# Router logits in pieces, W banks turned, and a new order of attention's work on five engines

## What is computed

```python
x = x + xattn(layernorm(x), ctx)          # q,k,v,o projections, softmax over 154 columns, 16 heads
h = layernorm(x)
w = softmax(h @ W_router.T + b_router)    # (tokens, 8)
w = keep_top_2(w)                         # the other six are zero
x = x + sum_e w[:, e] * (h @ W_experts[e].T + b_experts[e])
```

## Time and profile before

| what | us |
|---|---|
| median of three executions | 1285.32 |
| lowest, highest | 1275.66, 1287.61 |
| the profiled execution, first to last instruction | 1340.9 |
| PE busy in it | 1224.7 |
| DVE, ACT, POOL busy in it | 881.3, 722.1, 744.6 |
| one slot of attention in it, 175 to 220 us | 44.6 |
| one slot of attention in it, 420 to 471 us | 50.7 |

### The profile page before, as it was taken

The page is one execution under the profiler, slowest core; times in us unless marked ns, Lnnn a source line. Parts: engine busy times, 40 slices in busy tenths (PEclk is TensorE's granted clock), DMA queues, the critical chain, the costliest instruction groups (busy, mean ns, idle before and its releaser), DMA issues. The chain is left out here.

```text
span 1340.9 us, 36001 instructions
## 1 busy us (share of the span) xinstructions
PE 1224.7 (91%) x11024; PEld 735.1 (55%) x11025; DVE 881.3 (66%) x1933; ACT 722.1 (54%) x1040; POOL 744.6 (56%) x980
## 2 busy tenths in 40 slices
PE   8887999998999989999999986869899999999997
PEld 4445665655655655665655654534354555555454
DVE  4657787877868867867877867545445555555454
ACT  4336875775775775775766662624333333334333
POOL 4003555675675675675675674864644445444545
PEclk9879999999989998989989997889999999999999
DMA  8842664584583574583583573967999989998886
GB/s 267 253 135 65 173 176 153 148 254 142 150 258 130 142 241 152 147 262 131 144 237 115 132 215 109 357 221 156 199 177 184 175 173 188 179 172 155 168 165 133
DMA packets 135547, 239.22 MB, mean 178 GB/s; under 512 B 18440, under 2 KB 49416, under 8 KB 134280
## 3 DMA queue, kind: packets, MB, share of 16 engines
q1 hardware_dynamic: 102391, 161.24, 41.2%
q0 software_dynamic: 29808, 67.73, 25.2%
q10 hardware_dynamic: 3232, 8.68, 1.9%
HBM read 112.00 MB, written 101.40 MB: 159 GB/s over the span
## 5 line engine op out<-in xcount | busy, mean ns | idle before, releaser
L1854 PE MATMUL S<-we_s,wq_s 128*128 x1620 | 376.3, 382 | 12.6 <-DVE att L1832 5.8
L1782 POOL DMA_INDIRECT out<-xn,to x135 | 208.9, 1547 | 212.7 <-DMA out<-xn,to 123.6
L1854 PEld LDWEIGHTS S<-we_s,wq_s 128*128 128x128 f16 x1620 | 158.1, 98 | 180.8 <-issue 22.3
L1172 POOL TENSOR_TENSOR we_s<-P_s,we_s 128x1024 f16<-128x1024 f32 x96 | 204.2, 2136 | 65.6 <-ACT we_s L927 65.3
L1793 ACT ACTIVATE wq_s<-PVp 128x512 f16<-128x512 f32 x137 | 81.6, 597 | 272.4 <-PE PVp L1844 247.1
L1252 POOL DMA_INDIRECT dispatched<-xn,idx x128 | 131.7, 1029 | 92.6 <-ACT xn L620 52.1
L975 DVE TENSOR_REDUCE mx_sb<-S 128x6 f32<-128x924 f32 x160 | 171.3, 1111 | 11.3 <-PE S L726 9.1
L708 PE MATMUL W<-we_s,wq_s 128*128 128x512 f16 x512 | 168.7, 409 | 8.7 <-ACT mT L933 5.3
L746 PE MATMUL W<-wo_s,aT_hi 128*128 128x512 f16 x512 | 164.5, 383 | 2.6 <-DVE aT_lo L953 1.4
L1832 DVE SCALAR_TENSOR_TENSOR att<-S,be_s 128x512 f32<-128x512 f32 x135 | 93.3, 691 | 111.0 <-PE S L1854 101.5
L1810 DVE TENSOR_TENSOR wq_s<-PVp,wq_s 128x512 f16<-128x512 f32 x137 | 94.6, 691 | 38.3 <-ACT wq_s L1793 35.1
(11 more groups left out here) (207 smaller groups left out, 2039.8 us busy)
## 6 DMA issues: line engine op xcount, KB each, us to landing
P_s<-dispatched SPq DMA_DIRECT2D x139, 260.5 KB
we_s<-we_s SPq DMA_DIRECT2D x186, 128.0 KB, 6.0
be_s<-in_x SPq DMA_DIRECT2D x16, 1024.0 KB, 9.1
xR_s<-in_x SPq DMA_DIRECT2D x16, 1024.0 KB
out<-xR_s SPq DMA_DIRECT2D x16, 1024.0 KB
wst<-in_weT SPq DMA_DIRECT2D x16, 512.0 KB, 6.2
we_scratch<-wsp SPq DMA_DIRECT2D x16, 512.0 KB, 5.5
Kst<-k_scratch SPq DMA_DIRECT2D x16, 480.0 KB, 5.1
```

What stands on the lines that cost most here:

```text
L1172: e.tensor_tensor(Pst[1][:, r:r + 2, :], exps(n), Pst[0][:, r:r + 2, :], ALU.subtract).then_inc(pldp, 1)
L1782: e.indirect_dma_start(out, bass.IndirectOffsetOnAxis(ap=to[u][:, :], axis=0), yw[u % YW], None, bounds_check=N - 1, oob_is_err=False, com ...
L1854: m = e.matmul(Yp[:, u % 2, :], gT[u % 2][xp][:, k, :], we_s[:, bass.ds(n * WN + (wp * KC + k) * D, D)], start=(c == 0), stop=(c == 11))
```

## The change

- LA and LB are cut by token group into four pieces each (`pe_LA(e, b, j)`, `pe_LB(e, b, j)`). They write to columns 388 to 451 of the two PV banks, which PV leaves unused, in place of a W bank. They stand now between Q2 and MX3 of a slot: LB0, LA0, LB1, LB2, LB3 after Q2, LA1 and LA2 after MX2, LA3 after a step of O. LA is made one slot earlier.
- LA and LB leave `BANK` and `HOLDERS`; Q6, Q9 and the ATs swap their two W banks.
- New waits, since the banks are shared: LA0 and LB0 wait for a NM, PV4 for RA (`lae`), PV5 for the sum over LB's parts (`lbs`), which is a step of its own on DVE now (`dve_RL`), taken out of RB.
- The order of all five slot functions is written anew. No instruction's shape changes, and their number on PE stays.

```diff
 BANK = {
-    "ST0": 2, "ST1": 3, "ST2": 2, "Q9": 0, "AT0": 1, "ST3": 3, "AT1": 0, "ST4": 2, "LA": 1, "AT2": 1, "AT3": 0,
+    "ST0": 2, "ST1": 3, "ST2": 2, "Q9": 1, "AT0": 0, "ST3": 3, "AT1": 1, "ST4": 2, "AT2": 0, "AT3": 1,
...
-    "MX7": 3, "MX8": 2, "O9": 0, "MX9": 3, "MX10": 2, "MT": 1, "LB": 0, "Q6": 1,
+    "MX7": 3, "MX8": 2, "O9": 0, "MX9": 3, "MX10": 2, "MT": 1, "Q6": 0,
 }
...
+    def input_logits():
+        return PVp[:, 0, 388:388 + NJ * 2 * NE]
+
+    def output_logits(b):
+        return W[:, 1, 0:NJ * 2 * NE] if b.last else PVp[:, 1, 388:388 + NJ * 2 * NE]
+
+    def pe_LA(e, b, j):
+        before = b + (-2)
+        if j == 0:
+            e.wait_ge(t1e, b.at(4, 4))
...
+            elif before.here():
+                e.wait_ge(nmd, before.at(4, 2))
...
+    def pe_LB(e, b, j):
+        after = b + 1
+        if j == 0:
+            e.wait_ge(ate, b.at(4, 4))
...
+                e.wait_ge(nmd, after.at(4, 2))
...
+        if w == 4 and (b + 2).here():
+            e.wait_ge(lae, (b + 2).at(1, 1))
+        if w == 5 and (b + (-1)).here():
+            e.wait_ge(lbs, (b + (-1)).at(1, 1))
...
         if on_bp1:
-            pool_PL(e, bp1, 7)
             pool_PL(e, bp1, 8)
-        if on_b:
-            pool_BX(e, b, 3)
         if on_bm1 and bm1.here(NB - 3):
             pool_SC(e, bm1)
-        if on_b and not b.last:
+            pool_SD(e, bm1)
+        if on_b and (not b.last):
             pool_NC(e, b, 1)
             pool_RQ(e, b)
-        if on_bm1 and bm1.here(NB - 3):
-            pool_SD(e, bm1)
         if on_bp2:
             pool_PL(e, bp2, 0)
```

More of the change, by code:

```diff
@@ new lines, in pe_LB @@
+    def pe_LB(e, b, j):
+        after = b + 1
+        if j == 0:
+            e.wait_ge(ate, b.at(4, 4))
+            if b.first:
+                e.wait_ge(p_rx, 5)
+            if b.last:
+                e.wait_ge(x1s, b.at(4, 3))
+            else:
+                e.wait_ge(nmd, after.at(4, 2))
+        o = output_logits(b)[:, j * 2 * NE:(j + 1) * 2 * NE]
+        for k in range(KC):
+            e.matmul(o.rearrange("p (l e) -> p l e", l=2), aT[0][:, k, j * P:(j + 1) * P], wx_s[:, :, k, :], start=(k == 0), stop=False)
+        e.matmul(o[:, 0:NE], ones[:, :], cb_r[:, :], start=False, stop=False)
+        for k in range(KC):
+            m = e.matmul(o[:, 0:NE], aT[1][:, k, j * P:(j + 1) * P], wx_s[:, 0, k, :], start=False, stop=(k == KC - 1))
+        if j == NJ - 1:
+            m.then_inc(lbp, 1)
@@ L1408, in pe_slot @@
             pe_XT(e, bp2, 3, s)
-        if on_bm1 and not bm1.last:
+        if on_bm1 and (not bm1.last):
             pe_O(e, bm1, 3, s)
@@ L1462, in pe_slot @@
         if on_bp1:
+            pe_MX(e, bp1, 10, s)
+        if on_bm1 and (not bm1.last):
+            pe_O(e, bm1, 9, s)
+            pe_O(e, bm1, 10, s)
+            pe_O(e, bm1, 11, s)
+        if on_bp1:
             pe_MT(e, bp1, s)
-        if on_bm1 and not bm1.last:
-            pe_LB(e, bm1, s)
         if on_bp2:
@@ L1580, in dve_slot @@
             dve_ATl(e, bm2, 3)
+        if on_bm3 and (not bm3.last):
+            dve_RM(e, bm3)
         if on_bm1:
@@ L1588, in dve_slot @@
             dve_Oe(e, bm2, 0)
-        if on_bm3 and not bm3.last:
-            dve_RS(e, bm3)
+        if on_bm3 and (not bm3.last):
             dve_RE(e, bm3)
@@ L1593, in dve_slot @@
             dve_PL(e, bm1, 6)
-        if on_bm2:
-            dve_SN(e, bm2, 0)
+        if on_bm3 and (not bm3.last):
+            dve_RS(e, bm3)
         if on_bp1:
@@ L1598, in dve_slot @@
             dve_XTl(e, bp1, 2)
-        if on_bm3 and not bm3.last:
-            dve_RI(e, bm3)
-        if on_bp2 and not bp2.first:
+        if on_bp2 and (not bp2.first):
             dve_norm_var(e, 0, bp2)
@@ L1604, in dve_slot @@
             dve_XTl(e, bp1, 3)
+        if on_bm2:
+            dve_SN(e, bm2, 0)
         if on_bm1:
             dve_NM(e, bm1, 1)
-        if on_bm2 and not bm2.last:
+        if on_bm3 and (not bm3.last):
+            dve_RI(e, bm3)
+        if on_bm2 and (not bm2.last):
             dve_Oe(e, bm2, 1)
@@ L1617, in dve_slot @@
         if on_b:
+            dve_DMX(e, b, 1)
             dve_DMX(e, b, 2)
+        if on_bm2 and (not bm2.last):
+            dve_RL(e, bm2)
+        if on_bp1:
+            dve_RA(e, bp1)
+        if on_b:
             dve_DMX(e, b, 3)
@@ L1632, in dve_slot @@
             dve_DMX(e, b, 10)
-        if on_bm2 and not bm2.last:
+        if on_bm2 and (not bm2.last):
+            dve_Oe(e, bm2, 2)
             dve_Oe(e, bm2, 3)
@@ L1641, in pool_slot @@
             pool_PL(e, bp1, 2)
-        if on_bm1 and not bm1.last:
-            pool_RP(e, bm1)
-        if on_bp1:
-            pool_PL(e, bp1, 3)
         if on_b:
```

225 lines of the change are left out of this document (107 added, 118 removed).

## The result

| | median us | runs |
|---|---|---|
| before, on the chip of this comparison | 1281.82 | 1275.66 to 1287.61, 4 |
| after | 1349.68 | 1346.68 to 1350.62, 4 |

The ratio is 1.0535, with a 95% interval of 1.0485 to 1.0585. Forecast were 1290 us and a range of 1240 to 1309. The kernel before was then run beside the variants on five chips: 1281.7 us (median of 13) on chip 15, and 1333.4, 1327.0, 1338.0 and 1336.7 on chips 12, 1, 10 and 9. Ratios are therefore taken on one chip each.

The account below looks back on a forecast made before the run. PE was taken as busy nearly throughout, with PV0 then waiting for POOL's PL2. A slot of 15.0 + 31.5 = 46.5 us against 46.1 before, 12 x 0.4 = 5 us, gave 1290 us, range 1240 to 1309.

Parts of the forecast that it names:

- SP and MX0: MX0 ahead of Q0 and Q1: restacked q by 28.6 us after MT, MX0 at 28.2; up to 0.4 wait, counted 0.
- I count none after: Low clock (1.2 GHz level) in a slot after the change: none, against 1.0 us or so left before.
- the profile's cost: LB's stall in the scatter, 1.6 us plus 1.7 of low clock a slot: 40 of the 55.6 us over the median.
- the slot before, 46.1: Timed slot, MT to MT, before the change: profiled 50.7 less 55.6/12, about 46.1 us.
- The slot after, 46.5: Slot after the change: 15.0 us up to PV0 plus 31.5 from there to MT, without low clock.
- The part up to PV0: PE ready 13.6 us after MT, POOL's PL2 at 15.0; PV0 waits about 1.4 us for PL2.
- PE is not behind it now: On DVE, RB behind ATl1 takes a wait for RQ; PE was said not to stand behind RB.
- Rival 4: Slower: MX0 waits for the restacked q, 1.5 us a slot on top of the forecast, 1308 us; chance 0.18.
- The ends of the attention part: First slots: value rows wait for RA, one step, 0 to 1 us; after the slots LB keeps a W bank, 0.
- Rival 3: LB's stall is the chip's own, in timed runs too; moving LB frees 4.2 us a slot, 1235 us; chance 0.17.
- Rival 2: POOL is not late: scatter issues cost less unprofiled, PV0 goes at 13.6 us; 1267 to 1273 us; chance 0.20.
- WEl's new place: At the head of DVE's slot; if it misses the eight issues, PL2 and slot end 0.4 us earlier, 5 over 12 slots.

Follow-up runs that it names:

- group 1: Chip 15 and the chip of the result table, each met on one occasion, where the kernel before takes 1282 us.
- group 2: Chips 12, 1, 10 and 9, each met on one occasion, where the kernel before takes 1327 to 1338 us.
- b_again: The kernel before, unchanged, run once more with a profile on chip 12: 1334.72 us, span 1333.0.

## Why the prediction was wrong

- **The step that made the time wrong is in "SP and MX0": MX0's wait for the restacked q was "counted as 0"**, and with it the low clock ("I count none after"). Measured, in the eleven scattered slots, are 18.8 us of wait in 8 of them and 27.2 us at the 1.2 GHz level, half of them lost. The premise was that the scatter is over before KV. Its last issue is, but its packets run until 13.7 to 15.6 us after MT, the restack lands at 30.7 to 33.8 in the nine slots with an XA where 28.6 was the bound, and with the scatter half a slot later the wait is gone and 34.9 us with it.
- **A step that failed before that, without effect on the time, is the profile's cost.** I took the difference of 55.6 us between span and median for stall under the profile, and built the slot before, 46.1, from all of it, though the 3.3 us a slot that I could name make 40. A profiled execution takes as long as any, on one chip. By luck the slot came out nearly right for group 1: the kernel before has no trace there, but the same with the scatter moved takes 1.003 of its time and has slots of 46.0 us on average.
- **The slot after, 46.5, was short by 4.4 us**: 50.9 in eleven slots. The part up to PV0 was right: PV0 comes 15.45 us after MT in the mean (15.0 forecast), with Q6's wait at 0.35 with its signals (0.4) and the last issue of the scatter at 7.2 (7.1), though the ATs' wait took most of the time that PL2 was to cost. The error lies behind PV0: 35.5 us in the mean, where 31.5 was forecast. MX0's wait is 1.7 of these 4.0, XT0's and other waits 0.7, the low clock 1.0; the last 0.6 stand in no row as a wait.
- "PE is not behind it now", said of RB, was wrong. That the slot without a scatter takes 46.60, near the 46.5, is luck: without a scatter PE sets PV0, at 13.8 (13.6 forecast), and the sum is 45.1. Of its 2.0 us over 44.57, 1.3 are added waits, Q6's 0.3 and 1.4 of the ATs and XT0 for DVE behind RB's 3 us, less the 0.4 for RA; 0.7 stand in no row.
- **Rival 4 is the one that happened, and its price was too low**: 1308 us, at a chance of 0.18. MX0's wait is 18.8 us, 1.6 for each of 12 slots, as priced (1.5). What was missing is what came with it: 27.2 us at the 1.2 GHz level between 225 and 790, half of them lost, 1.2 a slot; five of these seven stretches begin within 1 us of MX0. The argument against the rival, that the scatter is over before KV, looked at POOL's issues only. The loads of SP are a part of it: without an XA the scattered slot takes 47.85. Whether XA's place in SP's order or the eight stores in one run made it so is not shown, since neither was moved alone in group 1.
- **The ends of the attention part were costed at 0 to 1 us.** The first MT came at 93.4 us, against 86.4 in the profile before and 85.5 in the kernel before with its scatter moved, some 7 us. Runs of group 2 point at two parts: SP's new order in the kernel before moved its first MT to 90.3, and MX0's old place in the changed kernel gave 89.3, 90.0 and 93.1, where that kernel itself had 93.5. The rest stays open.
- Rival 3 took the stall for the chip's own. It is, but of some chips: in group 2 the change does remove LB's and LA's "issue" idleness, and is still slower by 3.4%. Q8's and ST's signals and the chain of ACT and DVE up to AT2 now lie in the scatter, so PV0 comes 18.4 us after MT in the mean, where it comes at 13.8 without a scatter and came at 19.4 before the change (`b_again`), and the stretch behind it is 2.9 longer, with LA and LB in it. In group 1, as far as the later scatter on chip 15 shows, there was nothing to remove.
- Rival 2 is out: PV0 waited for POOL in 5 slots, and in no scattered slot does it come before 14.4. One reading behind it was wrong: POOL's work did not go through in 15 us before. PL2 ended 18.5 us after MT (436.64 and 2.13, less 420.29), with 3.8 us of POOL's idleness on the way.

The sum in group 1: attention from the first MT to the last takes 689.5 us with the order before (scatter moved), 716.4 with the new order (scatter moved), 751.3 with the change. The last of these is of another chip than the first two, taken for the same group. Of 61.8 us, 34.9 go with the scatter where the change has it and what it delays: in the eleven slots 18.8 of MX0's wait, 8.5 of low clock (half of 27.2 less half of 10.2), 4.1 of ST0's wait for MR, and some 3 more. The other 26.9 come with the rest of the order, 1.7 a slot in those eleven, 4.2 in the last and 3.5 in the first three. How they part into RB, Q6 and the ATs was not measured in group 1; nor was SP's order there, nor MX0's place alone. Why its chips show no stall, and whether PE shares with the scatter's packets a path for its records, its instructions or its signals, stays open.

The rule that I cited from the Trainium skill ("SBUF — State Buffer", section "Who interferes with whom"), a lock of the shared port for a whole instruction when VectorE reads two SBUF inputs and GpSimd reads SBUF, was applied to WEl and not to RB. RB's 0.69 us without and 3.03 and 4.32 us with a PL of 2.13 us beside it agree with it. By that rule each of RB's four small steps may wait for an instruction of POOL to end; the rows give the four together and do not show it step by step. The 0.4 us that WEl's new place was to be worth are not there in each slot: in the slot at 434.9 WEl runs from 438.78 to 439.97, and the issue at 439.50 takes 1.31 us.

## What to carry to other kernels

Before a trace's idle time is called a cost of the profile, run the kernel once more and compare the profiled time with the others of the same chip; a difference between two occasions is no property of either run. An indirect scatter is not over when its last issue is: here its packets moved for 7.8 us more, beside two loads of 1 MB. Count them, and ask which load on the critical path is issued meanwhile. Tiny two-input steps of DVE should not stand beside long POOL instructions on a chain that PE waits for; what that alone is worth here, no run shows.

## What the runs showed of the hardware

- The same kernel took 1276 to 1293 us on chip 15 and 1323 to 1344 on four others, each met once. A profiled execution was within 0.8% of the median of its kernel on its chip.
- On those four, narrow matmuls (LB at 26 ns each) stood in steps of 0.5 or 1.2 us from 2.2 us after a scatter's first packet to its last, 8.4 us for 0.93 of work, and a signal of PE came up to 7.3 us late. Matmuls of 512 columns ran on meanwhile. On chip 15 LB took 1.02 us beside a scatter's packets.
- A scatter of eight issues moved 640 packets, 2.13 MB. Its last packet ended 1.4 us after its last issue in the kernel before on chip 1 (612.0 against 610.6), and 7.8 us after it beside SP's loads in the changed kernel. The 1 MB load XA took 15.3 us to land beside it, and 10.7 with the scatter elsewhere.
- Four steps of DVE on 8 elements a row took 0.69 us alone and 3.03 to 4.32 beside POOL's elementwise work. An indirect issue took 1.3 to 2.2 us in 16 cases, each of them beside WEl (11 in the profile before, 5 in the one after), and 0.96 to 1.10 in all others.
